# Half a batch's context projected and normalised inside the last group of heads, and token layernorms finished on GpSimd

## What is computed

```python
def _L1_attn_ref(x, w_q, w_k, w_v, w_o):          # T = 1024, H = 16, D = 16
    q, k, v = (x @ w.T split into heads)
    q, k = _rope(q), _rope(k)
    scores = q @ k.T * SCALE
    scores = where(tok_mask, scores, -inf)         # causal, in blocks of 64
    ctx = softmax(scores) @ v
    return ctx @ w_o.T

def _L1_ffn_ref(x, w_gate, w_up, w_down):          # I = 1024
    h = silu(x @ w_gate) * (x @ w_up)
    h_sparse = _sparsify_2to4(h)                   # of four, the two of largest magnitude stay
    return h_sparse @ w_down
```

## Time and profile before

| | |
|---|---|
| timed runs, median of 3 (us) | 1753.75 (1753.49 to 1754.46) |
| profiled execution (us) | 1749.66 |
| its span (us) | 1747.8 |
| mean granted TensorE clock, of full speed | 0.917 |
| busy: PE, DVE, ACT, POOL (us) | 1479.3, 1146.7, 732.6, 219.9 |
| busy shares of the span | 85%, 66%, 42%, 13% |
| third phase, from about | 678 us |

### The profile page before, as it was taken

One profiled execution on the slowest core, in us unless ns is written; L12 is line 12 of the kernel. 1 busy time (PEld: TensorE's weight loads), 2 busy tenths in 40 slices (PEclk: granted clock), 3 DMA queues, 4 the chain that ended last, 5 costly groups with the idle time before them and its releaser, 6 DMA issues.

```text
span 1747.8 us, 25797 instructions
## 1 busy us (share of the span) xinstructions
PE 1479.3 (85%) x9682; PEld 826.3 (47%) x9683; DVE 1146.7 (66%) x2395; ACT 732.6 (42%) x1232; POOL 219.9 (13%) x225
## 2 busy tenths in 40 slices
PE   4999999967989983588878998887998788988796
PEld 2566666653657773223343533253533344433354
DVE  5566666636421135678668769668789578789475
ACT  5454444512212220426744137743147652157530
POOL 3344444411410001000000000100000100000000
PEclk8999999978999987759998979998989898989999
DMA  2000000005105412212101023111013111211000
GB/s 111 13 25 25 24 24 24 28 21 180 40 26 150 149 39 105 47 33 43 31 19 31 1 43 56 40 19 28 17 28 60 38 19 24 37 37 32 31 1 25
DMA packets 137483, 75.21 MB, mean 43 GB/s; under 512 B 117648, under 2 KB 126352, under 8 KB 136592
## 3 DMA queue, kind: packets, MB, share of 16 engines
q1 hardware_dynamic: 136800, 72.02, 16.8%
q0 software_dynamic: 576, 1.77, 0.4%
HBM read 37.59 MB, written 9.06 MB: 27 GB/s over the span
## 4 chain that ended last, share of the span: by engine, by line
issue 59%; POOL 2%; DVE 0%; POOLq 0%; DVEq 0%
POOL rs_sb L1443 1%; POOL ve_sb L1440 0%; POOL qks_sb L1457 0%; POOL v_sb L1455 0%; DVE bn_sb L1607 0%; DVE x_sb_sb L1622 0%; POOLq L1159 0%; POOLq L66 0%; POOL qks_sb L1447 0%; DVE mv_sb L1613 0%; DVEq L1159 0%; POOL v_sb L1454 0%; POOL qks_sb L1458 0%; DVE ident_h_sb L1803 0%; DVEq L66 0%
## 5 line engine op out<-in xcount | busy, mean ns | idle before, releaser
L1509 ACT ACTIVATE room_sb<-s_ps 128x1024 f32<-128x1024 f32 (+1 forms) x320 | 291.2, 941 | 167.1 <-PE s_ps L1965 162.5
L1674 DVE TENSOR_REDUCE mx_sb<-s_ps 128x1 f32<-128x512 f32 (+1 forms) x400 | 249.4, 649 | 63.5 <-PE s_ps L1941 40.2
L1938 PE MATMUL s_ps<-room_sb 48*128 48x512 f16 (+3 forms) x480 | 152.3, 354 | 30.6 <-DVE mx_sb L1669 16.3
L1985 PE MATMUL cm_ps<-room_sb,v_sb 128*32 128x512 f32 (+3 forms) x1536 | 166.2, 522 | 0.8 <-ACT room_sb L1515 0.8
L1965 PE MATMUL s_ps<-room_sb 51*128 51x128 f16 (+4 forms) x1152 | 150.4, 283 | 15.4 <-ACT room_sb L1509 10.6
L2080 PE MATMUL cm_ps<-w_fd_sb,room_sb 128*128 128x256 f32 x512 | 131.6, 405 | 14.6 <-DVE room_sb L1756 14.6
L1440 POOL TENSOR_TENSOR ve_sb<-mv_sb,eps_sb 128x4 f32<-128x4 f32 x24 | 5.0, 210 | 1027.9 <-DVE mv_sb L1613 1027.9
L396 DVE SCALAR_TENSOR_TENSOR x_sb_sb<-xp_sb,conv_w_sb,x_sb_sb 128x512 f32<-128x512 f32 x96 | 106.9, 1117 | 22.6 <-ACT x_sb_sb L319 20.5
L2067 PE MATMUL s_ps<-xbT_sb,w_fg_sb 128*128 128x512 f16 x384 | 107.3, 412 | 14.3 <-DVE ctok_sb L1722 12.7
L1938 PEld LDWEIGHTS s_ps<-room_sb 48*128 48x128 f16 x480 | 42.5, 95 | 161.7 <-DVE mx_sb L1674 85.0
L2080 PEld LDWEIGHTS cm_ps<-w_fd_sb,room_sb 128*128 128x128 f32 x512 | 97.2, 198 | 38.7 <-issue 14.3
(11 more groups left out here) (260 smaller groups left out, 2932.5 us busy)
## 6 DMA issues: line engine op xcount, KB each, us to landing
we_gu_sb<-we_gu SPq DMA_DIRECT2D x32, 352.0 KB
we_dn_sb<-we_dn SPq DMA_DIRECT2D x32, 176.0 KB
...
x_sb_sb<-rows SPq DMA_DIRECT2D x2, 2048.0 KB, 11.4
...
room_sb<-qks_sb SPq DMA_TRANSPOSE x88, 3.3
...
```

The lines of the kernel that those rows point to most:

```text
L1509: act.activation(weights[(g * NU + u) % SLOTS_P][:, 2 * pair:2 * pair + 2, 0:width(u) * P], W[s % 2][:, :, 0:width(u) * P], ACT.Exp, scale ...
L1674: dve.tensor_reduce(mx[:, pair, k % 2, slot:slot + 1], max_bank(g, m)[:, 0:count * P], AX.X, ALU.max, negate=True).then_inc(mx_ok, 1)
L1938: last = pe.matmul(bank[:, at * P:(at + plain) * P], query[head:head + NORM, i * P:(i + 1) * P], key[head:head + NORM, j * P:(j + plain) * ...
L1985: last = pe.matmul(O[32 * h:32 * h + 32, (i - half * GT) * P:(i - half * GT + count) * P], v[:, j, g * HG + h, :], weights[(g * NU + u) % ...
```

## The change

**The first half of the context.** In the last group of heads the first half's context is transposed in steps 10 and 11 (`first_context_transposed`, into `S[2]`), copied by VectorE alone, and projected in steps 13 to 16, one token tile a step. VectorE adds it in pairs of tiles and takes its statistics (`first_stats`), normalises it, and TensorE transposes it ahead of the last sums. Only the second half goes the old way, into `C` and `M`, and its projection stands behind the first gate and up product.

**The layernorms.** The statistics of the next batch's input move to the end of group 2, those of the previous batch's output to steps 3 and 6 of group 3, and the subtract-and-multiply of both goes to GpSimd (`on_pool`), as do all `x_low` but the first batch's. `ORDER` has the next batch's input first.

**Joined steps.** The two products of `rotate` with cosine and sine are one operation on a joined table; the eight operations of `count` are four.

```diff
         for b in range(NB):
+            if b + 1 < NB:
+                ORDER += [("x", b + 1, 0), ("x", b + 1, 1)]
             if b > 0:
                 ORDER += [("f", b - 1, 0), ("f", b - 1, 1)]
-            if b + 1 < NB:
-                ORDER += [("x", b + 1, 0), ("x", b + 1, 1)]
             ORDER += [("a", b, 0), ("a", b, 1)]
...
+        def on_pool(kind, b):
+
+            return kind == "x" and b > 0 or kind == "f" and b < NB - 1
...
         @block.gpsimd
+            def x_low(c, t):
+                k = c * ST + t
+                wait(pool, xs_high, k + 1)
+                xt_landed(pool, k - 2)
+                pool.tensor_tensor(xs[:, t % 2, 1, :], x_tile(c, t), xs[:, t % 2, 0, :], ALU.subtract).then_inc(xs_low, 1)
...
             for k in range(2, len(ORDER)):
                 kind, b, s = ORDER[k]
+                if (kind, s) == ("a", 0) and b + 1 < NB:
+                    x_low(b + 1, 0)
+                    x_low(b + 1, 1)
                 inverse_deviation(k)
-                if (kind, s) == ("a", 0) and b + 1 < NB:
-                    zero_columns(b + 1)
+                if on_pool(kind, b):
+                    wait(pool, rs_ok, k + 1)
+                    for t in range(GT):
+                        x = x_tile(b, s * GT + t)
+                        last = pool.tensor_scalar(x, x, mv[:, t, 0:1], rs[:, t:t + 1], ALU.subtract, ALU.mult)
+                    last.then_inc(ln_ok, 1)
+                if kind == "a" and b + 1 < NB:
+                    x_low(b + 1, 2 + s)
+                    if s == 0:
+                        zero_columns(b + 1)
+                    else:
+                        for t in range(4, ST):
+                            x_low(b + 1, t)
...
         @block.vector
+            def first_stats(b):
+                k = LN["a", b, 0]
+                wait(dve, mv_ok, k)
+                for t in range(GT):
+                    if t % 2 == 0:
+                        wait(dve, wo_mm, 3 * b + t // 2 + 1)
+                        own = x_sb[:, b * ST + t:b * ST + t + 2, :]
+                        dve.tensor_tensor(own, S[2][:, t // 2, :].rearrange("p (t c) -> p t c", t=2), own, ALU.add).then_inc(xr_ok, 1)
+                        wait(dve, xr_ok, 3 * b + t // 2 + 1)
+                    last = dve.bn_stats(bn[:, t, :], x_tile(b, t))
+                last.then_inc(bn_ok, 1)
+                wait(dve, bn_ok, k + 1)
+                wait(dve, ln_ok, k)
+                dve.sem_inc(passed, 1)
+                for t in range(GT):
+                    last = dve.bn_aggr(mv[:, t, :], bn[:, t, :])
+                last.then_inc(mv_ok, 1)
...
-                dve.tensor_tensor(ro[:, :, :], x, cos[:, t, :].unsqueeze(1).to_broadcast([P, 2 * HEADS, HD]),
+                wait(dve, rv_ok, k)
+                dve.tensor_tensor(rosn[:, :, :, :], x.unsqueeze(1).to_broadcast([P, 2, 2 * HEADS, HD]),
+                                  tables[:, :, t, :].unsqueeze(2).to_broadcast([P, 2, 2 * HEADS, HD]),
                                   ALU.mult).then_inc(turned, 1)
...
             def heads(b):
-                        if g == NHG - 1:
-                            if b > 0 and s in (2, 6):
-                                finish(b - 1, s // 4)
-                            if b + 1 < NB and s in (10, 14):
-                                layernorm("x", b + 1, s // 4 - 2)
-                if b + 1 < NB:
-                    x_low(b + 1, 0)
-                    x_low(b + 1, 1)
+                        if b + 1 < NB and g == NHG - 2 and s in (16, 18):
+                            stats("x", b + 1, s // 2 - 8)
+                        if b > 0 and g == NHG - 1 and s in (3, 6):
+                            wait(dve, f2_ok, 2 * b - 2 + s // 3)
+                            stats("f", b - 1, s // 3 - 1)
+                wait(dve, tc, 3 * b + 1)
+                dve.tensor_copy(xbT[:, 0, :, :], S[2][:, :, :]).then_inc(cTv_ok, 1)
+                first_stats(b)
+                normal("a", b, 0)
                 normalised(b, NHG - 1, 1)
...
         @block.tensor
+                        if g == NHG - 1 and s in (10, 11):
+                            first_context_transposed(b, s - 10)
+                        if g == NHG - 1 and 13 <= s < 17:
+                            out_projection(b, S[2], 0, s - 13)
...
                 weighted(b, NHG - 1, NU - 1, 0)
+                half_transposed(b, 0)
                 sums_transposed(b, NHG - 1, 1)
...
                     hidden(b, w, among_hidden)
+                    if w == 0:
+                        for t in range(GT):
+                            out_projection(b, CM, 1, t)
+                        if ahead:
+                            qkv(c, 1)
```

More of the change, by code:

```diff
@@ L1316, in sum_bank @@
         def sum_bank(g, half):
-            return RING[turns["sum", g, half] % 3]
+            return C if (g, half) == (NHG - 1, 1) else RING[turns["sum", g, half] % 3]
         def ring_bank_read(b, turn):
@@ L1853, in _ @@
                         low_parts(c, w + 1)
-                    if ahead and w + 4 < ST:
-                        x_low(c, w + 4)
                     if w >= 4 and w % 4 == 0:
@@ L2026, in heads, with first_context_transposed @@
                 weighted(b, NHG - 1, NU - 1, 0)
+                half_transposed(b, 0)
                 sums_transposed(b, NHG - 1, 1)
+            def first_context_transposed(b, f):
+                wait(pe, cn_ok, group(b, NHG - 1)(2, LEAD + 1))
+                if f == 0:
+                    wait(pe, mx_ok, group(b, NHG)(2 * NX, LEAD))
+                for t in range(GT):
+                    last = pe.transpose(S[2][:, f, t * P:(t + 1) * P], ctok[:, t, f * P:(f + 1) * P], ident[:])
+                if f == KD - 1:
+                    last.then_inc(tc, 1)
@@ L2029, in context_transposed @@
             def context_transposed(b):
-                wait(pe, cn_ok, 2 * NHG * b + LEAD + 2 * NHG)
-                for f in range(KD):
-                    for t in range(ST):
-                        last = pe.transpose(S[f][:, t // 4, (t % 4) * P:(t % 4 + 1) * P], ctok[:, t, f * P:(f + 1) * P], ident[:])
+                wait(pe, cn_ok, group(b, NHG - 1)(2, LEAD + 2))
+                for f, bank in enumerate((C, M)):
+                    for t in range(GT):
+                        last = pe.transpose(bank[:, t * P:(t + 1) * P], ctok[:, GT + t, f * P:(f + 1) * P], ident[:])
@@ L2118, in _ @@
                     pe.wait_ge(w_low, 4)
+                heads(b)
                 context_transposed(b)
[L2120 removed]
                 if ahead:
                     qkv(c, 0)
[L2123 to L2125 removed]
                 wait(pe, xTv_ok, 2 * b + 1)
```

118 lines of the change are left out of this document (47 added, 71 removed).

## The result

The changed kernel takes 1761.68 us (median of 6 runs, 1758.32 to 1770.38), the kernel before beside it 1752.95: a ratio of 1.0061, interval 1.0039 to 1.0082. It is slower by some 9 us (0.6%, and the interval leaves out 1), where 20 us less were forecast. The profiled execution has a span of 1760.4 us against 1747.8. That is 12.6 us, more than between the medians, since the profiled execution of the kernel before (1749.66) was 3.3 us under its median.

The account below looks back on a forecast made before the run. No engine is full: waits between stages, at the seams between batches, were taken to bound the kernel. 37.4 - 15.6 - 3.0 + 3.0 - 1.5 = 20.3 us less: 1729 profiled, 1733 median, range 1722 to 1746.

Parts of the forecast that it names:

- T: Layernorms on GpSimd: time of one 128x256 subtract-and-multiply there, taken as 0.5 us, bounds 0.46 and 0.8.
- The first context half is late by 12T - 5.25 us in two batches: VectorE's scaling ahead of the context transposes waits on GpSimd's normalisations; at 0.5 us each, 0.75 us late, twice.
- the GpSimd chain decides: Rival: GpSimd's normalisations delay the first context half, 16.2 us twice at 1.79 us each: 1764, slower; chance 0.05.
- Last group +4.4 us: Last group of heads: moved transposes and projection lengthen it from 9.1 to 13.5 us, weighted products ending 4.4 later.
- the wait for the scaling: Last group: TensorE waits some 0.5 us while VectorE scales the first half's sums.
- Seam of 7.0 and 5.1 us: Last weighted product to first gate product: 7.0 us, 5.1 in the last batch; with the longer group, gains together 37.4.
- Half-clock stretches are taken as gone: Seam: the forecast counted TensorE's stretches at half clock as removed.
- the clock stays low: Rival: TensorE's waits in the new order leave as much running at 1.2 GHz, 6.0 us: 1739; chance 0.16.
- Given back 4.5 us three times and 2.1: Behind the first gate product, the second half's projection delays the hidden products: 4.5 us in three batches, 2.1 last; total 15.6.
- Subtractions -3.0 us: VectorE's loop: moving subtractions to GpSimd saves at most 5.9 us but collides with VectorE; -1.0 a batch, -3.0 taken.
- Joined steps +3.0 (0 to 7): Sparsify steps and rotations: joining pairs of operations saves 3.0 us, bounds 0 and 7.
- The move: First context half's transposes and projection taken into the last group: 37.4 us gained less 15.6 given back, net 21.8.

Follow-up runs that it names:

- e8: Changed kernel with GpSimd's normalisation as two one-operation instructions (third batch's input) or two two-tensor instructions (fourth's); one run, 1770.23 us, only its trace used.
- e7: e5 plus ten matrix products without a use on TensorE in the seam, seven and three; 1731.45 us, ratio 0.9875 to the kernel before.
- e3: Changed kernel with the subtractions back on VectorE, GpSimd keeping the layernorms' second step; 1769.29 us, ratio 1.0074 to the kernel before.
- e5: Changed kernel, next batch's layernorms on VectorE behind the first context scaling, previous batch's on GpSimd at the third group's end, ScalarE's copies later; 1737.25 us, ratio 0.9904.
- e6: Changed kernel with nothing new on GpSimd: moved half and joined steps only, layernorm steps in VectorE's waits, ScalarE's copies later; 1737.49 us, ratio 0.9918.
- e4: Kernel before with the joined small steps alone (rotation's products in one instruction, counts' eight additions in four); 1747.34 us, ratio 0.9960.

## Why the prediction was wrong, point by point

- **The step that failed: T.** "It reads one tensor, like the copy, so I take 0.5", bounded by 0.8. It is 1.226 us (L1484), and e8 shows why the likeness misled: on GpSimd the form with a scalar a partition takes 0.93 us for 256 columns with one operation, more than two tensors with one (0.61). The nearest row by columns and inputs was not the nearest by form. Nor was L220 "the same operation on 4 columns": in the kernel it is one operation, a maximum with a constant, and has no scalar a partition. My upper bound was no bound: it scaled the two-input row by columns as if that were the dearest form. The Trainium skill, GPSIMD Engine Reference, "3.1 Elementwise — side-by-side cycle accounting", gave 0.45 by estimate, from its 1.03 cycles an element; the 1.226 of the trace decides, and the page's estimate is further off than my value.
- **The mechanism was right.** "The first context half is late by 12T - 5.25 us in two batches": with 1.226 that is 9.46 us; the wait was 9.83 in both batches, against 0.35 in the first batch, so 9.48. The rival "the GpSimd chain decides" had it, with 0.05 of the chance and the turning point at T of about 1.5. The point lay lower, because other terms were short too: with T at 1.226 the prediction's own sum still gives 20.3 + 1.5 - 18.9 = 2.9 us less than before. That the rival's 1764 lies near the measured 1762 is luck, for it took T as 1.79.
- **The clock behind the wait.** TensorE stood 9.83 us and came back at a granted clock of 0.50, so the stretch grew by 11.6 and 11.1 us, not 9.5: together 3.7 us. The fourth batch, with two links, lost 0.95.
- **Last group +4.4 us.** +4.9 where the chain is not late (14.9 against 10.0); the wait for the scaling, taken as 0.5, is 0.35 to 0.49. Right.
- **Seam of 7.0 and 5.1 us.** 7.65 and 5.5 at full clock, 10.0 twice at 0.66. "Half-clock stretches are taken as gone" failed. The rival "the clock stays low" was true of three seams in four (0.66, 0.66 and 0.75); e7 shows its price in the two, 2.4 us each. The seams lost 46.6 us against 55.0 forecast.
- **Given back 4.5 us three times and 2.1.** 5.3 us at the first hidden product less 0.35 at the second, so 5.0; in the last batch 6.3, of which 3.4 come back by the sixteenth, so 2.9. The total is 17.8 where 15.6 were taken.
- **Subtractions -3.0 us.** The lock of the earlier trace rows is seen, 0.35 us a turn, but a turn still gets 0.28 shorter (5.24 to 4.96). The Trainium skill, SBUF — State Buffer, "Who interferes with whom", holds in these rows (0.77 against 0.42, and 1.40 against 0.67 on GpSimd), but the lock is no measure of the loss. By the turn the sign was wrong and the size small; in the whole time nothing shows: e3 and the changed kernel do not differ clearly, nor e5 and e6.
- **Joined steps +3.0 (0 to 7).** 7.0 in e4, of which its trace places 3.7.

The miss by the two profiled spans is 12.6 + 20.3 = 32.9 us: about 24 in the last groups (chain and the clock behind it), 8 in the seams, 2 given back, and -2 in the rest. T alone makes 17.4 of the 24.

The move was priced too high even without the chain. It was forecast at 37.4 - 15.6 = 21.8 us; with the last group's 14.9 us in every batch, as in e7, the table leaves 46.6 us from the seams less 19.8 for the last groups and 17.8 given back, 9.0 us, and e6 against e4 leaves some 7. That e5 and e6 (1737) came within 5 us of the forecast of 1733 is luck in part: 7.0 of their 15 us are the joined steps.
